# A six-layer network on one core: the attention product moved to the scores' PSUM banks, and every engine's order laid out anew

## What is computed

```python
for i in range(DEPTH):                       # 6
    x = attn_layer(shift_tokens(x), Wqkv[i], q_scale[i], k_scale[i], Wo[i]) + x
    x = ffn_layer(shift_tokens(x), ln_g[i], ln_b[i], W1[i], b1[i], W2[i], b2[i]) + x
# attn_layer: q, k, v = split(x @ Wqkv), 16 heads of 64
q = l2norm(q) * qs; k = l2norm(k) * ksc      # then rotary with a scale
sim = einsum('bhwie,bhwje->bhwij', bq, bk2) * 8.0   # windows of 32, each sees itself and the one before
attn = softmax(where(mask, -max, sim)); out = einsum('bhwij,bhwje->bhwie', attn, bv2)
return out @ Wo
# ffn_layer: layernorm(x) @ W1 + b1 -> a, gate; a * gelu(gate) @ W2 + b2   (341 wide)
```

## Time and profile before

| | |
|---|---|
| median of 3 runs | 2231.51 us (2224.43 to 2232.05) |
| profiled execution | 2231.53 us, span 2229.8 us |
| PE busy | 1949.5 us, 87% of the span |
| DVE | 1347.5 us, 60% |
| ACT | 1181.8 us, 53% |
| POOL | 1198.6 us, 54% |
| mean granted TensorE clock | 0.965 of full speed |
| DMA | 125.09 MB, mean 56 GB/s |

### The profile page before, as it was taken

One profiled execution on the slowest core, in us unless ns is written; L12 is line 12 of the kernel. 1 busy time (PEld: TensorE's weight loads), 2 busy tenths in 40 slices (PEclk: granted clock), 3 DMA queues, 4 the chain that ended last, 5 costly groups with the idle time before them and its releaser, 6 DMA issues. The chain is left out here.

```text
span 2229.8 us, 70852 instructions
## 1 busy us (share of the span) xinstructions
PE 1949.5 (87%) x30532; PEld 1195.8 (54%) x30632; DVE 1347.5 (60%) x1564; ACT 1181.8 (53%) x2030; POOL 1198.6 (54%) x1291
## 2 busy tenths in 40 slices
PE   6868998899899889899988989999898899986898
PEld 5635555555455555555555555555555555553444
DVE  5647666666666666566665666666666666653443
ACT  4426555655555555465555556555555655653234
POOL 0229665675665576566666566756665665650000
PEclk8979999999999999999999999999999999998788
DMA  1023222322222222222222213222232222221000
GB/s 43 1 91 76 56 59 50 86 58 62 58 57 55 70 66 68 50 59 73 66 56 66 59 47 87 56 65 57 57 77 60 69 64 55 48 55 43 0 10 10
DMA packets 84767, 125.09 MB, mean 56 GB/s; under 512 B 26208, under 2 KB 31976, under 8 KB 84336
## 3 DMA queue, kind: packets, MB, share of 16 engines
q1 hardware_dynamic: 84464, 120.64, 21.5%
HBM read 21.98 MB, written 1.05 MB: 10 GB/s over the span
## 5 line engine op out<-in xcount | busy, mean ns | idle before, releaser
L320 POOL TENSOR_TENSOR qkn<-t 128x1024 f32<-128x1024 f32 x192 | 451.8, 2359 | 195.9 <-PE ring L392 118.5
L311 POOL TENSOR_TENSOR qkn<-qkn,rn 128x512 f32<-128x512 f32 x384 | 388.2, 1042 | 7.5
L392 PEld LDWEIGHTS ring<-ident,qkn 128*128 128x128 f32 x1536 | 181.7, 142 | 311.7 <-issue 265.1
L392 PE MATMUL ring<-ident,qkn 128*128 128x128 f32 x1536 | 237.9, 278 | 68.8 <-ACT gel L609 34.2
L440 PE MATMUL ring<-prT,v_win 64*64 64x32 f32 x12288 | 241.3, 222 | 64.5 <-issue 63.5
L440 PEld LDWEIGHTS ring<-prT,v_win 64*64 64x64 f32 x12288 | 213.7, 136 | 156.2 <-issue 144.6
L684 DVE TENSOR_REDUCE den<-pexp 128x16 f32<-128x1024 f32 x96 | 117.1, 1220 | 258.9 <-ACT pexp L546 258.9
L704 DVE TENSOR_TENSOR t<-qk_ps,rot 128x1024 f32<-128x1024 f32 x192 | 228.7, 1191 | 70.2 <-ACT sq L576 62.0
L328 POOL TENSOR_TENSOR pn<-pexp,rden 128x512 f32<-128x512 f32 x192 | 196.2, 1043 | 120.7 <-DVE rden L689 120.5
L670 DVE TENSOR_REDUCE smax<-sc_ps 128x16 f32<-128x1024 f32 x96 | 117.6, 1225 | 231.3 <-PE sc_ps L409 231.3
L370 PE MATMUL qk_ps<-wqkv,state 128*128 128x512 f32 x384 | 224.4, 669 | 14.4 <-DMA wqkv<-in_w_qkv 8.0
(11 more groups left out here) (238 smaller groups left out, 2910.5 us busy)
## 6 DMA issues: line engine op xcount, KB each, us to landing
v_win<-v_tok SPq DMA_DIRECT2D x1488, 64.0 KB
wqkv<-in_w_qkv SPq DMA_DIRECT2D x18, 512.0 KB, 3.8
wo<-in_w_o SPq DMA_DIRECT2D x6, 512.0 KB, 3.7
w<-in_w SPq DMA_DIRECT2D x6, 341.0 KB, 3.3
w<-in_w SPq DMA_DIRECT2D x6, 192.0 KB, 3.1
r_xtok<-in_x SPq DMA_DIRECT2D x4, 256.0 KB, 3.7
amask<-in_att_mask SPq DMA_DIRECT2D x1, 1024.0 KB
out_x<-xo SPq DMA_DIRECT2D x4, 256.0 KB, 2.3
```

Source lines behind the costliest of these rows:

```text
L311: nc.gpsimd.tensor_tensor(by_head(quarter(qkn, f)), by_head(quarter(qkn, f)), rn[:, 8 * f:8 * (f + 1)].unsqueeze(2).to_broadcast([P, 8, DH ...
L320: nc.gpsimd.tensor_tensor(half(qkn, k), half(t1, k), half(t2, k), ALU.add).then_inc((q_added, k_added)[k], 1)
L392: ins = nc.tensor.transpose(to[:, n * P:(n + 1) * P], qkn[:, c * P:(c + 1) * P], ident[:, :])
```

## The change

The attention product is written to `sc_ps`, after the scores in it have been read by the subtraction of the row maximum (`sc_sub`); the next scores wait until ACT has copied it out (`oT_copied`). The ring loses its two fills. TensorE, ACT, DVE and POOL each get a new order: k and v are projected first and q late; POOL scales q and k in the stage that projects them, in the order 1, 3, 0, 2, and the turns run in the order 1, 3, 2, 0 in the next. DVE rotates only after ACT has squared. SP waits, ahead of a tile's v DMAs, for the attention product three tiles back. The mask is unchanged. `stage_fills` is rewritten to follow TensorE's order and is left out here, as are the small changes of helpers in the same sense (`state_there` repeats the wait for x_ffn).

```diff
-        STAGES = TILE_COUNT + 6
+        STAGES = TILE_COUNT + 7
+        turn_at = {f: n for n, f in enumerate((1, 3, 2, 0))}
+        scale_at = {f: n for n, f in enumerate((1, 3, 0, 2))}
...
+                    if g > 2:
+                        sp.wait_ge(av_full, g - 2)
...
+                    pool.wait_ge((q_added, k_added)[f // 2], g + 1)
...
-                        pool.wait_ge(qkT_full, 4 * (g - 1) + 2 * (k + 1))
+                        pool.wait_ge(qkT_full, 4 * (g - 1) + max(turn_at[2 * k], turn_at[2 * k + 1]) + 1)
...
-                    if tile_there(g - 1):
-                        inverse_norms(g - 1)
-                        for f in range(4):
-                            scale_qk(g - 1, f)
                     if tile_there(g - 2):
-                        for f in range(2):
-                            scale_p(g - 2, f)
+                        scale_p(g - 2, 0)
+                        scale_p(g - 2, 1)
                     if tile_there(g):
-                        for k in range(2):
-                            add_terms(g, k)
+                        add_terms(g, 1)
+                        add_terms(g, 0)
+                        inverse_norms(g)
+                        scale_qk(g, 1)
+                        scale_qk(g, 3)
+                        scale_qk(g, 0)
+                        scale_qk(g, 2)
...
-                        if g > 0:
-                            pe.wait_ge(sc_sub, 2 * g)
+                        if g == 1:
+                            pe.wait_ge(sc_sub, 2)
+                        if g > 1:
+                            pe.wait_ge(oT_copied, 2 * (g - 1))
...
-                        for part in range(2):
-                            ring_bank("a", g, part)
+                        pe.wait_ge(sc_sub, 2 * min(g + 2, TILE_COUNT))
...
-                                        to[part][64 * par:64 * (par + 1), P * pair + WIN * q:P * pair + WIN * (q + 1)],
+                                        sc_ps[64 * par:64 * (par + 1), part, P * pair + WIN * q:P * pair + WIN * (q + 1)],
...
-                    now, turn, prob, att = (tile_there(g - n) for n in range(4))
-                    up, down = round_at(g, 0, 2), round_at(g, 1, 2)
-                    out_0, out_1, centre = round_at(g, 1, 1), round_at(g, 2, 1), round_at(g, 3, 1)
-                    for f in range(2):
-                        if att:
-                            attend(g - 3, f)
-                        if now:
-                            project_q(g, f)
+                    out_0 = round_at(g, 1, 1)
+                    out_1 = round_at(g, 2, 1)
+                    centre = round_at(g, 3, 1)
+                    spread = round_at(g, 3, 1)
+                    up = round_at(g, 0, 2)
+                    down = round_at(g, 1, 2)
+                    if tile_there(g):
+                        project_k(g, 0)
+                        project_k(g, 1)
+                        project_v(g, 0)
+                        project_v(g, 1)
+                    if tile_there(g - 3):
+                        attend(g - 3, 0)
+                    if tile_there(g - 1):
+                        transpose_qk(g - 1, 1)
+                    if up is not None:
+                        ffn_up(up, 0)
                     if centre is not None:
                         ffn_centre(centre)
-                    if turn:
+                    if tile_there(g - 3):
+                        attend(g - 3, 1)
+                    if tile_there(g - 1):
+                        transpose_qk(g - 1, 3)
+                    if tile_there(g):
+                        project_q(g, 1)
+                    if tile_there(g - 1):
+                        transpose_qk(g - 1, 2)
                         transpose_qk(g - 1, 0)
+                    if tile_there(g):
+                        project_q(g, 0)
+                    if up is not None:
+                        ffn_up(up, 1)
+                    if tile_there(g - 2):
+                        transpose_p(g - 2, 0)
                     if down is not None:
                         ffn_down(down)
-                    if now:
-                        project_k(g, 0)
-                    if turn:
-                        transpose_qk(g - 1, 1)
-                    if now:
-                        project_k(g, 1)
-                    if up is not None:
-                        ffn_up(up, 0)
-                    if turn:
-                        transpose_qk(g - 1, 2)
-                    if now:
-                        project_v(g, 0)
-                    if up is not None:
-                        ffn_up(up, 1)
-                    if turn:
-                        transpose_qk(g - 1, 3)
+                    if tile_there(g - 1):
+                        scores(g - 1, 0)
+                    if out_1 is not None:
+                        output_projection(out_1, 1)
+                    if tile_there(g - 2):
+                        transpose_p(g - 2, 1)
                     if out_0 is not None:
                         output_projection(out_0, 0)
-                    if centre is not None:
-                        ffn_variance(centre)
-                    if now:
-                        project_v(g, 1)
-                    if out_1 is not None:
-                        output_projection(out_1, 1)
+                    if spread is not None:
+                        ffn_variance(spread)
                     if up is not None:
                         ffn_up(up, 2)
-                    for f in range(2):
-                        if prob:
-                            transpose_p(g - 2, f)
-                        if turn:
-                            scores(g - 1, f)
+                    if tile_there(g - 1):
+                        scores(g - 1, 1)
...
-                    nc.scalar.copy(oT[:, 4 * f:4 * f + 4, P * t:P * (t + 1)], bank_of("a", g, f)).then_inc(oT_copied, 1)
+                    nc.scalar.copy(oT[:, 4 * f:4 * f + 4, P * t:P * (t + 1)], sc_ps[:, f, :]).then_inc(oT_copied, 1)
...
-                    if k == 0:
-                        act.wait_ge(q_rot, 2 * (g + 1))
-                    else:
-                        act.wait_ge(k_full, 2 * (g + 1))
+                    act.wait_ge((q_full, k_full)[k], 2 * (g + 1))
...
-                    now, turn, prob, att = (tile_there(g - n) for n in range(4))
-                    up, centre = round_at(g, 0, 2), round_at(g, 3, 1)
-                    for f in range(2):
-                        if prob:
-                            exponentials(g - 2, f)
-                        if att:
-                            copy_o(g - 3, f)
+                    centre = round_at(g, 3, 1)
+                    spread = round_at(g, 3, 1)
+                    up = round_at(g, 0, 2)
+                    if tile_there(g):
+                        squares(g, 1)
+                        copy_v(g, 0)
+                        copy_v(g, 1)
+                    if tile_there(g - 2):
+                        exponentials(g - 2, 0)
+                        exponentials(g - 2, 1)
+                    if tile_there(g - 1):
+                        copy_qkT(g - 1, 1)
                     if centre is not None:
                         centred(centre)
-                    for f in range(2):
-                        if turn:
-                            copy_qkT(g - 1, f)
-                    if now:
-                        squares(g, 1)
                     if up is not None:
                         gelu(up, 0)
-                    if turn:
+                    if tile_there(g - 3):
+                        copy_o(g - 3, 0)
+                    if tile_there(g - 1):
+                        copy_qkT(g - 1, 3)
+                    if tile_there(g - 3):
+                        copy_o(g - 3, 1)
+                    if tile_there(g - 1):
                         copy_qkT(g - 1, 2)
-                    if now:
-                        copy_v(g, 0)
+                        copy_qkT(g - 1, 0)
+                    if tile_there(g):
+                        squares(g, 0)
                     if up is not None:
                         gelu(up, 1)
-                    if turn:
-                        copy_qkT(g - 1, 3)
-                    if now:
-                        squares(g, 0)
-                    if centre is not None:
-                        inverse_deviation(centre)
-                    if now:
-                        copy_v(g, 1)
+                    if tile_there(g - 2):
+                        copy_pT(g - 2, 0)
+                        copy_pT(g - 2, 1)
                     if up is not None:
                         gelu(up, 2)
                         nc.scalar.preload_act_table_set(LN_EXP_SET)
-                    for f in range(2):
-                        if prob:
-                            copy_pT(g - 2, f)
-                    if now:
+                    if spread is not None:
+                        inverse_deviation(spread)
...
```

(45 more changed lines are left out.)

76 lines of the change are left out of this document (36 added, 40 removed).

## The result

The changed kernel takes 2058.98 us (median of 4 runs, 2051.16 to 2059.67) against 2228.64 beside it, a ratio of 0.923 with an interval of 0.920 to 0.926. Its profiled execution has a span of 2057.6 us against 2229.8. The forecast was 2135, 2085 at best: the sign was right, the gain far too small.

The account below looks back on a forecast made before the run. TensorE sets the pace, at 77.5 us a round; 67.4 + 1.2 + 1.2 + 1.2 = 71.0 in the new order. So 2231.5 - 156 + 60 at the layers = 2135.5, put at 2135 us, range 2085 to 2195.

Parts of the forecast that it names:

- TensorE's work in the new order: TensorE's matmuls over four stages, counted from start to start: 17.89, 18.84, 16.26 and 14.45, together 67.4 us a round.
- plus the unexplained 0.3 a stage, 1.2: TensorE time in the old stage left without explanation, carried into the new order: 1.2 us a round.
- I take 1.2: TensorE issue idle left in the new order: 1.2 us a round, between bounds of 0 and the old 3.3.
- My sum: ... 1.2 a round: TensorE's waits for other engines in the new order, by stage 0.7, 0.2, 0.1 and 0.2 us, or 1.2 a round.
- (a): Attention product waits for the row maximum's subtraction, done 2.8 us into the stage while k and v run: costs nothing.
- (b): Scores wait for both copies of oT, which ACT does by 9.4 us; scores are due at 11: free.
- (e): At stage 1 the second output half waits 0.15 us for the state's update, which needs the down matmuls.
- (c): Scaling of q and k moved to the projections' stage; in stage 3 its chain just fits before the next turns.
- The change of layer: SP's in-order queue loads wv late, so TensorE stands 8.5 us; 12.0 us net with a clock dip, five times: 60 us.
- The clock outside the changes of layer: Four half-speed stretches of 7 us, each costing 3.5; fewer stalls should save two of them, 7 us.
- Rival 2: Order misses TensorE's floor as scaled quarters come late, margin 0.2 us after stage 3: 2229 us, 0.08; half, 2182, 0.14.
- rival 3: Instruction supply stalls each attention half by 0.86 us, 6.9 a round in place of 1.2: 2269 us, chance 0.06.

Follow-up runs that it names:

- the second profile: The unaltered changed kernel, run again on the chip of two runs with reordered weight loads: 2060.93 us, ratio 0.919 to the kernel before.
- The two experiments with SP's order: Changed kernel with wv loaded ahead of the v copies, 2018.25 us; and with wk, wv, wq all loaded as early as their data allow, 2008.6 us.
- the kernel before with the banks and the pause alone: Kernel before, attention product in the scores' banks, TensorE projecting q and k ahead of it, other engines' orders old: 2363.01 us, ratio 1.057.

## Why the prediction was right or wrong

- **TensorE's work in the new order: right.** 67.4 us by the sum of starts to starts; the round took 68.1, with waits of some 1 us.
- **"plus the unexplained 0.3 a stage, 1.2": wrong, worth 1.2 us a round.** I carried it over from the old stage without asking what it was. The timeline of the kernel before shows it in the same stage that the earlier trace rows come from: a first attention half with a stall in it,

```profile
1018.68 0.90 PE L440 MATMUL ring<-prT,v_win 64*64 64x32 f32 x48
...
1020.81 0.70 PE L370 MATMUL qk_ps<-wqkv,state 128*128 128x512 f32 x1
```

  takes 2.13 us from start to start in place of 1.07. It lost 1.06, of which the profile calls 0.86 idle; the other 0.2 is the pipeline's end, busy in the rows and lost all the same. In this stage, two thirds of the "unexplained" were a part of the stall, and had to go with it. How it is in other stages was not worked out; but the changed kernel shows nothing of the 1.2.
- **"I take 1.2" for the issue idle: wrong, worth 1.1 a round.** 1.2 us in the attention over the whole span are left (2.2 in the second profile). The step argued from long passes ahead of the attention and from the v copies' traffic. The copies have nothing to do with it (0.998, and 1.9 us of idle with the copies laid over half of it). The pause matters (63.5 to 10.7), and so do the four transposes between the halves (16.2 us without them), which the step didn't see. Nor did it see what became of the scores: their halves had only p1 between them, and in the changed kernel long passes stand there in every stage with a feed-forward, an output half in this stage 2:

```profile
942.54 0.86 PE L417 MATMUL sc_ps<-kT,qT 64*32 64x64 f32 x64
943.33 3.72 PE L462 MATMUL ring<-oT,wo 128*128 128x256 f32 x16
946.89 0.60 PE L431 MATMUL ring<-ident,pn 128*128 128x128 f32 x4
947.42 0.86 PE L417 MATMUL sc_ps<-kT,qT 64*32 64x64 f32 x64
```

  Their 15.1 us became 0.6, while the three kernels that kept the scores' old place kept 18.3 to 20.3. That this spacing did it was not tried by itself. The lower bound, 0, was the answer.
- **"My sum: ... 1.2 a round" for the other waits: right in size.** Stage 0 took 19.00 for a sum of 18.6 with its waits, stages 1 to 3 0.3 to 0.4 less than their sums with waits, 19.04, 16.36 and 14.65. The gelu's wait went from 1.5 to 0.2 a round, as walked. (a), (b) and (e) cost nothing measurable. (c), "it just fits", was nearly exact: 9.5 us of waits for POOL, all behind a stage 3, some 0.6 each, and 1.1 us more work costs 1.2 us there.
- **The change of layer: right in mechanism, 10.4 in place of 12.0 us.** k0 waited 2.3, v0 6.5 (8.8 together, forecast 0.8 and 8.5), and the clock fell behind it each time. The forecast charged the dip with 3.4 us; part of it passes while TensorE is idle, and about 2 remain. The two experiments with SP's order show that all of it comes from the loads that stand behind q0's late end and behind 14 copies in one queue.
- **The clock outside the changes of layer: right in sign, half the size.** "Fewer stalls should save two of the four, 7 us". In the kernel before, each of the four stretches begins within 2 us of the end of a fetch stall of 1.3 to 1.7 us (1.70, 1.32, 1.44 and 1.46), and they last 27 us, which at half speed cost 14. In the changed kernel, between 300 and 1800 us, the clock falls at the five changes of layer alone.
- **The sum.** Predicted gain 156 and loss 60; measured 224 and 52, since 172 came off the span. The difference in the gain, 68, is 71.0 - 68.1 = 2.9 us a round, 64 us over the 22 full rounds, and 7 from the clock, less 3 at the start and end of the pipeline. The 2.9 are these two allowances, 2.3, and 0.6 from the sum of work and waits. So the step that failed is the adding of the two allowances: both were taken from the old order, they were in part one cost counted twice, and nearly nothing of either survived. Order and mechanism were right, and the size of the gain wrong by them.
- **The rivals.** None came about. Rival 2's margin behind a stage 3 was real and rival 3's mechanism exists, but not in this order. The range of 2085 left the case of no stalls at all outside, at 71.0 - 2.4 = 68.6 a round, 2079: that case deserved more than the 0.15 that its half was given.

What stays open: which rule decides whether a burst outruns the fetches. The adjacent halves, 128 products in 2.07 us, stall in 14 of 96 stages; the scores of the kernel before, with p1 between them, do in 28 stages. Nor is the pause ahead of the product the whole of it: with its halves adjacent, 3.7 us of long passes ahead left 16.2, 22.0 and 34.1 us of idle in three kernels, and 1.9 us of them left 10.7. Where in the stage the fetch of a block begins was not varied.

## What to carry to other kernels

Idle that the profile gives to nothing ("issue") has a cause too: set it beside the instruction fetches, and count its price from start to start, since a stall of 0.86 us lost 1.06. A measured remainder of the old order may not be added to a new one until it is known what it is made of. And when a step is moved on one engine, follow every queue that waits for it: q's new place cost 10.4 us a layer through SP, which a new order of three loads gave back.

## What was new of the hardware

- Of 388 issue stalls of TensorE over 0.25 us in thirteen traces, 372 ended 1.10 to 1.61 us after the end of a 16 KB instruction fetch. Nearly all came in runs of small matmuls, 64 in 1.07 us or faster, and DMA traffic beside them made no difference.
- The granted clock falls in stretches with many short gaps too, not behind a long one alone: in the kernel before with the banks and the pause alone the commonest waits of the rounds are of 0.7 to 2.8 us in the mean and 2.9 at most, and 99 of the 1450 us from 300 on pass at the lower level (27 in the kernel before). That the gaps are the cause was not tried by itself.
